# Last stage of a layer-norm, channel-mixing and expert kernel: four row buffers of the statistics in four partition groups, smaller weight loads, another ScalarE order

## The reference, cut to what matters

```python
xn = layer_norm(x, norm_a, norm_b)
left = (xn @ Wl + bl) * jax.nn.sigmoid(xn @ Wlg + blg)
right = (xn @ Wr + br) * jax.nn.sigmoid(xn @ Wrg + brg)
out_gate = jax.nn.sigmoid(xn @ Wog + bog)
out = jnp.einsum('bkjd,bkid->bijd', left, right) / n
out = layer_norm(out, on_a, on_b) * out_gate
out = out @ Wo + bo
...
x = x + out
t = t + _L0_ffn_ref(_ln_t(t), gate_w, gate_b, weight1, weight2)
...
logits = jnp.einsum('bsd,ed->bse', x, gate_w) + gate_b
probs = jax.nn.softmax(logits, axis=1)
vals, idx = jax.lax.top_k(probs.transpose(0, 2, 1), K)
...
h = jax.nn.gelu(jnp.einsum('ebd,edh->ebh', h, weight1), approximate=False)
out = jnp.einsum('ebh,eho->ebo', h, weight2)
```

## Time and profile before

| what | value |
|---|---|
| median of 3 runs | 3088.07 us (3087.18 to 3091.25) |
| the profiled execution, its own time | 3078.97 us |
| its span | 3077.0 us |
| PE, DVE, ACT, POOL busy | 84%, 79%, 77%, 61% |
| stage 3, from the trace | about 1893 to 2958 us |
| loads and stores of a step of stage 3 | four of 512 KB, one of 36 KB |
| first FFN weight on ScalarE's queue | 16 loads of 1024 KB |
| mean DMA rate over the span | 284 GB/s |

### The profile page before, as it was taken

The page is one execution under the profiler, slowest core; times in us unless marked ns, Lnnn a source line. Parts: engine busy times, 40 slices in busy tenths (PEclk is TensorE's granted clock), DMA queues, the critical chain, the costliest instruction groups (busy, mean ns, idle before and its releaser), DMA issues.

```text
span 3077.0 us, 66113 instructions
## 1 busy us (share of the span) xinstructions
PE 2588.5 (84%) x14998; PEld 2145.9 (70%) x15070; DVE 2428.7 (79%) x4824; ACT 2363.5 (77%) x4284; POOL 1889.3 (61%) x2343
## 2 busy tenths in 40 slices
PE   7999999999999989989998984777777777777735
PEld 6888888888888878888988983555555555555523
DVE  6777777777777769999999996778777787787862
ACT  6888888888888877887878872888778787787850
POOL 8888888888888860000000003888788887887842
PEclk9999999999999999999999996999999999999967
DMA  5777777777777769999999985888888888888836
GB/s 199 270 267 268 267 270 273 270 269 269 267 268 268 270 256 318 333 327 325 343 330 325 332 295 185 301 309 307 297 300 309 303 299 298 309 309 297 303 139 202
DMA packets 281154, 873.00 MB, mean 284 GB/s; under 512 B 29223, under 2 KB 81602, under 8 KB 281122
## 3 DMA queue, kind: packets, MB, share of 16 engines
q1 hardware_dynamic: 272322, 855.31, 77.2%
q10 hardware_dynamic: 8448, 16.78, 1.6%
q0 software_dynamic: 352, 0.53, 0.2%
HBM read 492.97 MB, written 379.52 MB: 284 GB/s over the span
## 4 chain that ended last, share of the span: by engine, by line
PE 43%; DMA 17%; issue 14%; POOL 12%; DVE 5%; ACT 4%; SPq 2%; POOLq 1%; ACTq 0%; another core or an unknown queue 0%; DVEq 0%
PE banks L1267 32%; DMA arena<-left_d 11%; POOL rs L693 5%; DMA statrow<-stat_d 5%; POOL arena L664 4%; PE banks L1256 4%; PE banks L1335 3%; ACT arena L809 2%; PE banks L1301 1%; ACT work L879 1%; DVE left_parts L1006 1%; PE banks L1326 1%; PE banks L1336 1%; SPq L475 1%; DVE arena L1014 1%
## 5 line engine op out<-in xcount | busy, mean ns | idle before, releaser
L1267 PE MATMUL banks<-x_parts,w_parts 128*128 128x512 f32 x4320 | 1068.3, 399 | 0.8 <-POOL x_parts L626 0.8
L1267 PEld LDWEIGHTS banks<-x_parts,w_parts 128*128 128x128 f32 x4320 | 791.9, 189 | 162.9 <-POOL x_parts L626 1.2
L1301 PE MATMUL banks<-left_parts,right_parts 128*128 128x384 f32 x3456 | 629.3, 341 | 67.2 <-ACT arena L810 56.8
L1301 PEld LDWEIGHTS banks<-left_parts,right_parts 128*128 128x128 f32 x3456 | 606.2, 191 | 90.5 <-issue 86.0
L957 DVE SCALAR_TENSOR_TENSOR arena<-banks,cols,arena 128x512 f32<-128x512 f32 x576 | 406.6, 747 | 255.7 <-ACT arena L775 252.3
L879 ACT ACTIVATE work<-arena,nmr,rs 128x128 f32<-128x128 f32 x1152 | 458.9, 482 | 151.9 <-POOL nmr L695 145.5
L659 POOL COPY rcol<-late 128x8 f32 (+1 forms) x144 | 28.4, 197 | 722.3 <-ACT late L825 722.3
L664 POOL TENSOR_TENSOR arena<-arena,work 128x512 f32<-128x512 f32 x288 | 359.7, 1270 | 163.1 <-DVE arena L1063 161.9
L1335 PE MATMUL banks<-wo_sb,arena 128*128 128x128 f32 x2304 | 413.3, 309 | 0.1
L1335 PEld LDWEIGHTS banks<-wo_sb,arena 128*128 128x128 f32 x2304 | 373.6, 200 | 29.4 <-issue 1.8
L626 POOL TENSOR_TENSOR x_parts<-xn,x_parts 128x512 fp32r<-128x512 f32 x288 | 372.2, 1292 | 6.6 <-ACT x_parts L763 6.6
(11 more groups left out here) (177 smaller groups left out, 4459.5 us busy)
## 6 DMA issues: line engine op xcount, KB each, us to landing
arena<-in_x_dram SPq DMA_DIRECT2D x144, 512.0 KB, 3.4
left_d<-arena SPq DMA_DIRECT2D x144, 512.0 KB, 2.6
right_d<-arena SPq DMA_DIRECT2D x144, 512.0 KB, 3.4
gate_d<-arena SPq DMA_DIRECT2D x144, 512.0 KB, 4.2
arena<-right_d SPq DMA_DIRECT2D x128, 576.0 KB, 5.8
arena<-left_d SPq DMA_DIRECT2D x128, 576.0 KB, 6.8
mixed_d<-arena SPq DMA_DIRECT2D x128, 576.0 KB, 4.2
work<-mixed_d SPq DMA_DIRECT2D x144, 512.0 KB, 4.2
```

What stands on the lines that cost most here:

```text
L1267: last = nc.tensor.matmul(ps[2 + k][:, :], w_parts[:, wq, k], x_parts[:, xq, b, c], start=((wq, xq) == TERMS[0]), stop=((wq, xq) == TERMS[ ...
L1301: last = nc.tensor.matmul(ps[NT * b + t][:, 0:GRID], lr_parts[RIGHT][:, rq, b, k, t * P:(t + 1) * P], lr_parts[LEFT][:, lq, b, k], start=( ...
```

## The change

Four things are edited, all in stage 3.

1. `statrow` gets four buffers, each in a group of 32 partitions of its own (rows 32r to 32r+17 for step 4j+r). `coef` is loaded four times, once into each group. The products L1326 and L1336 take only the 18 rows of the group, with a tile position (32r, 0); in the compiled program they have a tile size of 32 x 128 in place of 128 x 128. Their number, their columns and their order among the other products stay.
2. `load_parts` waits for the step four before and is issued three steps ahead. SP and PE loop over four steps at a time (`quads`).
3. `exponentials` comes right after `scale_rest` on ScalarE.
4. The first FFN weight is loaded in 28 pieces of 512 KB at 28 cuts of ScalarE's loop, and 4 pieces after it.

```diff
         body(i)
...
+def quads(engine, steps, body, drain=0):
+    last = steps // 4 - 1
+    body(0)
+    with engine.Fori(1, last) as j:
+        body(j)
+    for j in range(last, steps // 4 + drain):
+        body(j)
...
+def shifted4(j, r, k):
+    return j + (r + k) // 4, (r + k) % 4
...
+def in_range4(j, r, k, steps):
+    return not isinstance(j, int) or 0 <= 4 * j + r + k < steps
...
+def halves_of(j, r):
+    return 2 * j + r // 2, r % 2
...
         expo = sb("expo", [P, CHUNK])
-        statrow = sb("statrow", [P, 2, 2, CHUNK], BF16)
+        statrow = sb("statrow", [P, 2, CHUNK], BF16)
...
-            def load_parts(i, b):
-                s = 2 * i + b
-                sp.wait_ge(s_z3, mark(2, s - 2, 2))
+            def load_parts(j, r):
+                s = 4 * j + r
+                if not isinstance(j, int) or j > 0:
+                    sp.wait_ge(s_z3, mark(2, s - 4, 2))
                 settle(sp, s_tick_sp)
-                sp.dma_start(statrow[0:KR, b], stat_r[s].broadcast_to([PARTS, 2 * PARTS, 2 * CHUNK])).then_inc(s_sin[b], 16)
+                sp.dma_start(statrow[BAND * r:BAND * r + KR], stat_r[s].broadcast_to([PARTS, 2 * PARTS, 2 * CHUNK])).then_inc(s_sin[r], 16)
...
-            def stage3(i):
-                for b in range(2):
-                    if in_range(i, b, 2, STEPS):
-                        load_mixed(*shifted(i, b, 2))
-                    if in_range(i, b, -1, STEPS):
-                        store_result(*shifted(i, b, -1))
-                    if in_range(i, b, 1, STEPS):
-                        load_x3(*shifted(i, b, 1))
-                    if in_range(i, b, 2, STEPS):
-                        load_parts(*shifted(i, b, 2))
+            def stage3(j):
+                for r in range(4):
+                    if in_range4(j, r, 3, STEPS):
+                        load_parts(*shifted4(j, r, 3))
+                    if in_range4(j, r, 2, STEPS):
+                        load_mixed(*halves_of(*shifted4(j, r, 2)))
+                    if in_range4(j, r, -1, STEPS):
+                        store_result(*halves_of(*shifted4(j, r, -1)))
+                    if in_range4(j, r, 1, STEPS):
+                        load_x3(*halves_of(*shifted4(j, r, 1)))
...
             sp.wait_ge(s_stst, 16 * 2 * PARTS)
-            load_parts(0, 0)
-            load_parts(0, 1)
-            pairs(sp, STEPS, stage3, drain=1)
+            for r in range(3):
+                load_parts(0, r)
+            quads(sp, STEPS, stage3, drain=1)
...
             pool.wait_ge(s_setup, 3)
-            for a in range(PARTS):
-                pool.dma_start(coef[2 * PARTS * a:2 * PARTS * (a + 1), :, :], exact_p[:, a]).then_inc(s_coef, 16)
+            for r in range(BANDS):
+                for a in range(PARTS):
+                    at = BAND * r + 2 * PARTS * a
+                    pool.dma_start(coef[at:at + 2 * PARTS, :, :], exact_p[:, a]).then_inc(s_coef, 16)
...
             def load_w1(n):
-                for j in range(2 * n, 2 * n + 2):
-                    act.dma_start(w1_sb[:, j], w1_view[j]).then_inc(s_w1, 16)
+                j, first = n // 2, BANDS // 2 * (n % 2)
+                some = slice(first, first + BANDS // 2)
+                act.dma_start(w1_sb[:, j, some], w1_view[j, :, some]).then_inc(s_w1, 16)
...
                         scale_rest(i, b)
+                    if in_range(i, b, -4, STEPS):
+                        exponentials(*shifted(i, b, -4))
                     if in_range(i, b, -1, STEPS):
...
                         copy_transposed(*shifted(i, b, -2))
-                    if in_range(i, b, -4, STEPS):
-                        exponentials(*shifted(i, b, -4))
-            cuts = [lambda n=n: load_w1(n) for n in range(WLOADS - 1)]
+            cuts = [lambda n=n: load_w1(n) for n in range(4 * (WLOADS - 1))]
             pairs(act, STEPS, stage3, drain=2, cuts=cuts)
...
                 act.wait_ge(s_ost[b], 16 * (STEPS // 2))
-            load_w1(WLOADS - 1)
+            for n in range(4 * (WLOADS - 1), 4 * WLOADS):
+                load_w1(n)
             act.wait_ge(s_nm, 1)
...
-            def outer(i, b):
-                s = 2 * i + b
-                pe.wait_ge(s_sin[b], 16 * (i + 1))
+            def outer(j, r):
+                s, rows = 4 * j + r, slice(BAND * r, BAND * r + KR)
+                pe.wait_ge(s_sin[r], 16 * (j + 1))
                 for h in range(2):
                     pe.wait_ge(s_w3, mark(2, s - 1, h + 1))
-                    nc.tensor.matmul(ps[h][:, :], coef[:, 0, :], statrow[:, b, h, :], start=True, stop=True).then_inc(s_c3, 1)
-            def project(i, b):
-                s = 2 * i + b
+                    nc.tensor.matmul(ps[h][:, :], coef[rows, 0, :], statrow[rows, h, :], start=True, stop=True,
+                                     tile_position=(BAND * r, 0)).then_inc(s_c3, 1)
+            def project(j, r):
+                s, b, rows = 4 * j + r, r % 2, slice(BAND * r, BAND * r + KR)
                 for h in range(2):
...
                         nc.tensor.matmul(ps[2 + h][:, tok], gated[:, b, h, tok], wo_sb[:, :], start=True, stop=False)
-                        last = nc.tensor.matmul(ps[2 + h][:, tok], statrow[:, b, h, tok], coef[:, 1, :], start=False, stop=True)
+                        last = nc.tensor.matmul(ps[2 + h][:, tok], statrow[rows, h, tok], coef[rows, 1, :], start=False, stop=True,
+                                                tile_position=(BAND * r, 0))
                     last.then_inc(s_z3, 1)
...
-            def stage3(i):
-                for b in range(2):
-                    if in_range(i, b, 1, STEPS):
-                        outer(*shifted(i, b, 1))
-                    if in_range(i, b, 0, STEPS):
-                        project(i, b)
-                    if in_range(i, b, -3, STEPS):
-                        logits(*shifted(i, b, -3))
-                    if in_range(i, b, -2, STEPS):
-                        transposes3(*shifted(i, b, -2))
+            def stage3(j):
+                for r in range(4):
+                    if in_range4(j, r, 1, STEPS):
+                        outer(*shifted4(j, r, 1))
+                    if in_range4(j, r, 0, STEPS):
+                        project(j, r)
+                    if in_range4(j, r, -3, STEPS):
+                        logits(*halves_of(*shifted4(j, r, -3)))
+                    if in_range4(j, r, -2, STEPS):
+                        transposes3(*halves_of(*shifted4(j, r, -2)))
             pe.wait_ge(s_rtc, NT * NT)
-            pe.wait_ge(s_coef, 16 * PARTS)
+            pe.wait_ge(s_coef, 16 * PARTS * BANDS)
             pe.wait_ge(s_setup, 3)
             outer(0, 0)
-            pairs(pe, STEPS, stage3, drain=2)
+            quads(pe, STEPS, stage3, drain=1)
...
             pe.wait_ge(s_pl, 1)
-            pe.wait_ge(s_w1, 16 * SIDE)
+            pe.wait_ge(s_w1, 16 * 2 * SIDE)
```

More of the change, by code:

```diff
@@ L351, in build @@
         s_x3 = [sem(f"s_x3{b}") for b in range(2)]
-        s_sin = [sem(f"s_sin{b}") for b in range(2)]
+        s_sin = [sem(f"s_sin{r}") for r in range(BANDS)]
         s_rc = sem("s_rc")
@@ L593, in _ @@
             alone(nc.gpsimd.memset(pick_row[:, :, :], -1.0))
-            alone(nc.gpsimd.memset(statrow[:, :, :, :], 0.0))
+            alone(nc.gpsimd.memset(statrow[:, :, :], 0.0))
             alone(nc.gpsimd.memset(coef[:, :, :], 0.0))
```

## The result

| | before | the change |
|---|---|---|
| median of 4 runs each | 3089.5 us (3087.2 to 3091.3) | 3346.0 us (3329.3 to 3351.1) |
| ratio, 95% interval | | 1.082 (1.078 to 1.086) |
| profiled execution, its span | 3079.0, 3077.0 us | 3351.1, 3349.2 us |
| stage 3, first to last start of the reciprocal deviation | 1056.0 us, 7.385 a step | 1325.5 us, 9.269 a step |

The change makes the kernel 8.2% slower, far above the range of 2970 to 3140 us and the 3101 forecast. The whole of it is in stage 3: 1325.5 - 1056.0 is 269.5 us, and the spans differ by 272.2.

The account below looks back on a forecast made before the run. Waits, no full resource, bounded stage 3; TensorE would become the bound: 143 steps at 7.42 us make 1061 against 1056, +5, and +8 for the start, so +13 on the 3088 median: 3101 us, range 2970 to 3140.

Parts of the forecast that it names:

- Four buffers, an earlier load: Stage 3: the row gets two more steps to land, so the 169.4 us of `outer` waits go, with a smaller gain.
- Rival E: SP reaches the early load late and `outer` still waits: about 3088 us, folded into "within 0.2%" (0.11 in all).
- Exponentials first: ScalarE, stage 3: exponentials fall into the wait of `normalise` for POOL, worth 0.35 us a step where that loop decides.
- 28 pieces: Weight loads, stage 3: 512 KB pieces remove TensorE's 5.04 us wait for the row; 21 more cuts cost nothing.
- What comes next if only these count: Stage 3 without the 18-row cost: POOL 6.28, DMA 6.35, loop 6.55 us a step, taken together as 6.65.
- The loop that I priced at 6.55: Stage 3's two-step loop through exponentials, `logits`, gate, scales and `normalise`: 6.90 - 0.35 = 6.55 us a step.
- The products on 18 rows: TensorE, stage 3: tile size changes cost 0.25 us a pair, 0.12 at `outer`; step 5.30 + 2.12 = 7.42 us.
- Rival A: The 18 rows cost nothing, a pair stays at 0.33 us: 2990 us (2960 to 3025), chance 0.30.
- +8 us for the start: Start of stage 3, partly at 1.2 GHz: TensorE, which waited there, now fills it, about one step more.
- the case itself: The forecast's main case, TensorE bound at 7.42 us a step: 3080 to 3140 us, chance 0.52.
- my upper bound: TensorE, stage 3: each product waits for the whole one before, 0.76 us a pair, 8.7 us a step.
- D: Rival nearer the upper bound, from 7.7 us a step; at 8.7 the result is 3275 us; chance 0.08.

Follow-up runs that it names:

- four_rows32: full_rows with its narrow products (in `outer` and `project`) cut to rows 0 to 31, tile size 32 x 128: 3334.2 us.
- turned: The changed kernel with every second pair of `project` turned round, row product first, 18 rows kept: 2935.6 us; with rounds 2938.0 us, ratio 0.953.
- full_rows: The changed kernel with its four buffers along the free dimension and those products over all 128 rows again: 2937.0 us, ratio 0.951.
- run 6: full_rows with those products cut to rows 0 to 65, tile size 128 x 128 as their neighbours: 2933.2 us.
- four_rows18: full_rows with those products cut to rows 0 to 17, tile size 32 x 128, without the partition groups: 3371.3 us.

## Why the prediction was wrong

**Four buffers, an earlier load: right.** The wait of 169.4 us is gone in every run with them. Rival E is out. The prediction said that the gain would be less than those 169 us; it is about 81.

**Exponentials first: right, and close.** Forecast 0.35 us a step, measured 6.81 - 6.41 = 0.40.

**28 pieces: right in kind.** No step at a load is near 12 us any more. The 21 more issues show no loss; the whole is worth 17 us in the version that isn't bound by TensorE (2954.0 to 2937.0).

**What comes next if only these count: 6.65 us forecast, 6.41 measured.** Two of the limits were sized well, POOL 6.28 (busy 772.31 of 800 us over 124.9 steps, 6.18) and the DMA 6.35 (share 0.97, 350 GB/s; 2.24 MB / 350 GB/s = 6.40). The addition "with three limits so close I take 6.65" was too much by 0.24 us, 35 us of the time. The loop that I priced at 6.55 had more slack.

**The products on 18 rows, at full clock: right mechanism, nearly the right size.** A pair was forecast at 0.58 us and takes 0.575: 0.42 us from the fp32 product to the narrow one (0.28 before), 0.15 back (0.05 before). TensorE's step was forecast at 7.42 us and takes 7.17 at full clock. The part by part count of the rows above is 0.53 (`outer`) + 8 x 0.575 + 1.01 (`logits`) + 1.03 (transposes) = 7.17. Against 5.30 + 2.12 the pairs lack 0.16 us, mostly because the last row product of a step hands over to `logits` with a change of tile size in the kernel before too (0.15 us), and I charged it again. (Of the prediction's own terms, 7 x 0.33 + 0.28 is 2.59 and not 2.61; nothing hangs on it.) The rest is 0.06 at the transposes and 0.03 at `outer`. That TensorE drains when the tiling mode changes is what the Trainium skill says ("TensorEngine Tiling", section "Key Properties"); the trace agrees for groups of rows now, with 0.24 us for the two changes of a pair. That one product with 32 rows takes the time of one with 128 is what the Trainium skill says in "TensorE: Matmul & The Clock Gate", section "Why this matters for your kernels"; `four_rows32` agrees for a product's own duration (0.23 us against 0.22), and the pace of a pair shows that it doesn't hold for such products between full ones. Rival A, a pair at 0.33 us, is out.

**The step that failed is that TensorE was priced at full clock alone.** The prediction has "its clock is full nearly throughout" and a stage with +8 us for the start. With 64 rows, where that holds, the sum is nearly right: 143 x 7.22 = 1033 us in place of 1061, and 3056 us measured, 45 below the forecast, inside the range as a whole and below the 3080 to 3140 of the case itself. In the change the granted clock of stage 3 is 0.73 and adds 290 us. No rival had a clock that falls while TensorE is busy. I had two rows for the lower level before me, the start of stage 3 with 0.81 and a pair of `outer` products of 1.03 us in place of 0.60, and used them for the start only. The trace had the price of a pair in `project` at that level too, 0.65 us from start to start in place of 0.33, with no change of tile size:

```profile
1894.62 0.74 PE L1335 MATMUL banks<-wo_sb,arena 128*128 128x128 f32 x2
1895.27 0.74 PE L1335 MATMUL banks<-wo_sb,arena 128*128 128x128 f32 x2
```

A TensorE that bounds the step makes each fall of the clock count in full: a step wholly at the lower level takes 12.6 us here (the third of the stage, PEclk 0.50), more than the 8.7 of my upper bound, and a pair takes 0.94 us there, past the 0.7 that I had named as a sign of being wrong. D had the right sign, but another mechanism: its price was a wait of each product for the one before it, and pairs at full clock never show that. The start cost 13 us in place of 8 (the first five steps take 49.0 us, 5 x 7.17 are 35.9; with 64 rows it is 44.7 us, 9 more).

**What stays open.** Why the clock falls. The runs show that it falls with sixteen changes of tile size a step and 18, 32 or at times 34 rows; that with the rest of the edit in place it doesn't with 48 or more rows, nor with 18 rows and nine changes, past the start of the stage; and that in the kernel before 66 rows without a change of tile size lower it a little (0.90 against 0.97). Neither theory of the expectations holds alone: the changes alone would have brought it down with 64 rows, the rows alone would have left it down in `turned`. TensorE's busy share doesn't tell these cases apart, being 800 of 800 us with 18, 34, 48 and 64 rows. Nor does it at the start of the stage: from 1893 to 1926 us TensorE is busy for all 33 us at a clock of 0.50 in the change and of 0.57 with 64 rows, and for 27.7 us at 0.90 in `full_rows`. No run varied the number of changes without changing which products stand side by side, and none held the pace of the step while it changed the order; that rows and pace act together is untested.

## What to carry to other kernels

Four buffers and an earlier load are bought cheaper on the free dimension, or with the narrow products placed side by side: with the rest of the edit the first gives 2937 us and the second 2938, about 5% below the kernel before, and both run into POOL and the DMA. When a change makes TensorE the bound, price its step at both levels of the clock, and look at PEclk in windows of a few steps before all else. Between products on 128 rows, a product narrow enough to change the tile size isn't free though it lasts no longer (66 rows kept 128 x 128 and cost nothing in run 6, 64 didn't): count the changes of tile size, and count those that were there before.

## What the runs showed of the hardware

- Two changes of tile size in a pair took it from 0.33 to 0.575 us, the same for 18 and for 64 rows: 0.14 us into the narrow product, 0.10 out of it, and each weight load starts only with its own product. At the lower level of the clock the pair takes 0.94 us, and 0.65 without a change.
- With TensorE busy for 740 of 740 us the granted clock was 0.73 (18 rows, sixteen changes a step), for 800 of 800 us it was 1.00 (64 rows), and for 797 of 800 us it was 1.00 (18 rows, nine changes).
- A loop can hold two patterns for the same program: with 34 rows stretches of about 75 us at a clock of 1.00 and 7.18 us a step and stretches of about 167 us at 0.71 and 9.4 us a step take turns.
- Where the clock falls first isn't fixed: the change ran seven steps at 7.14 to 7.18 us before it fell, `four_rows18`, with the same products on other partitions, had no such stretch.
